# Third and fourth pass: gathered rows split into three bf16 parts on chip, summed by bf16 products

## The reference

```python
# layer 2 (third pass); ci, cj from the out and in degrees
msg = feat[src] * ci[src, None]
agg = segment_sum(msg, dst, N) * cj[:, None]
h = agg @ weight + bias
# layer 3 (fourth pass)
h = x @ W
msgs = h[src] * edge_weight[:, None]
y = segment_sum(msgs, dst, N) + bias        # then a layernorm with gamma, beta
```

## Time and profile before

| What | Value |
|---|---|
| time, median of 3 runs | 4434.95 us (4428.1 to 4437.35) |
| profiled execution, its span | 5246.3 us |
| first pass, first to last gather issue | 42.0 to 1410.5 us |
| second pass | 1471.2 to 2717.4 us |
| third pass | 2809.2 to 3997.5 us |
| fourth pass | 4024.9 to 5213.1 us |
| busy: PE, DVE, ACT, POOL | 52%, 38%, 26%, 61% of the span |

### The profile page before, as it was taken

How to read it: one execution, slowest core, us unless ns; L and a number is a source line. 1 busy time by engine, 2 the same in 40 slices (tenths; PEclk the granted TensorE clock), 3 DMA queues, 4 the chain that set the end, 5 groups by cost and what they waited for, 6 DMA issues and landing times.

```text
span 5246.3 us, 56090 instructions
## 1 busy us (share of the span) xinstructions
PE 2714.9 (52%) x15042; PEld 2473.5 (47%) x15042; DVE 1982.1 (38%) x4498; ACT 1353.8 (26%) x4318; POOL 3200.4 (61%) x3366
## 2 busy tenths in 40 slices
PE   6666676666756666566683543332334333333334
PEld 6666676666645555556552432222224222222234
DVE  3555545555655555555554111111113221122124
ACT  1121112222333333333343321211112121111113
POOL 4555555556356666666646666666665666666664
PEclk7676666767777777777785555555555555555555
DMA  7655555555433333333321111111112111111111
GB/s 193 156 142 140 148 137 139 149 143 144 125 94 85 81 84 83 82 83 83 83 60 42 35 35 35 35 35 35 35 35 46 35 36 34 35 35 34 35 35 44
DMA packets 337349, 409.90 MB, mean 78 GB/s; under 512 B 212224, under 2 KB 248691, under 8 KB 336957
## 3 DMA queue, kind: packets, MB, share of 16 engines
q0 software_dynamic: 133120, 245.58, 19.7%
q1 hardware_dynamic: 203933, 160.75, 11.7%
HBM read 386.26 MB, written 19.77 MB: 77 GB/s over the span
## 4 chain that ended last, share of the span: by engine, by line
another core or an unknown queue 32%; PE 19%; DVE 15%; POOL 14%; issue 14%; ACT 3%; DMA 1%; SPq 1%; ACTq 0%; DVEq 0%; POOLq 0%
POOL rows L563 14%; PE bank L655 10%; DVE same L1557 3%; DVE first_only L1256 2%; PE bank L669 2%; DVE first_only L1395 2%; DVE same L1256 2%; PE bank L668 1%; DVE prod L1325 1%; DVE score L1327 1%; DVE prod L1323 1%; PE bank L752 1%; DVE first_only L1264 1%; PE bank L759 1%
## 5 line engine op out<-in xcount | busy, mean ns | idle before, releaser
L655 PE MATMUL bank<-same,rows 128*96 128x128 f32 x4992 | 1059.8, 385 | 1468.8 <-issue 540.6
L655 PEld LDWEIGHTS bank<-same,rows 128*96 128x96 f32 x4992 | 917.5, 246 | 1593.7 <-issue 866.8
L563 POOL DMA_INDIRECT rows<-kv_table,src_idx x832 | 789.7, 949 | 610.0 <-DVE msg L1335 357.0
L563 POOL DMA_INDIRECT rows<-pair_table,src_idx x832 | 786.4, 945 | 520.5 <-issue 208.6
L563 POOL DMA_INDIRECT rows<-h_table,src_idx x832 | 788.7, 948 | 426.9 <-issue 235.0
L938 ACT COPY acc<-bank 96x511 f32 (+1 forms) x832 | 479.4, 576 | 2205.1 <-remote 1582.2
L563 POOL DMA_INDIRECT rows<-ci_table,src_idx x832 | 785.0, 943 | 412.6 <-issue 239.1
L1256 DVE TENSOR_TENSOR same<-bank,rank_col 128x512 f32<-128x512 f32 x624 | 420.6, 677 | 1000.7 <-remote 587.9
L1557 DVE TENSOR_SCALAR same<-iota_s,rank_col,src_hi 128x128 f32<-128x128 f32 x832 | 235.0, 359 | 906.7 <-remote 748.2
L655 PE MATMUL bank<-same,msg 128*105 128x128 f32 x1664 | 366.3, 391 | 384.5 <-ACT acc L940 362.7
L655 PEld LDWEIGHTS bank<-same,msg 128*105 128x105 f32 x1664 | 321.8, 268 | 398.2 <-DVE same L1256 200.9
(11 more groups left out here) (168 smaller groups left out, 2899.5 us busy)
## 6 DMA issues: line engine op xcount, KB each, us to landing
first_only<-in_attr_cols SPq DMA_DIRECT2D x104, 384.0 KB
first_only<-q_table SPq DMA_DIRECT2D x832, 48.0 KB
first_only<-rank_rows SPq DMA_DIRECT2D x104, 256.0 KB
first_only<-keep_rows SPq DMA_DIRECT2D x104, 192.0 KB
rows<-kv_table,src_idx POOLq DMA_INDIRECT x832
rows<-pair_table,src_idx POOLq DMA_INDIRECT x832
rows<-ci_table,src_idx POOLq DMA_INDIRECT x832
rows<-h_table,src_idx POOLq DMA_INDIRECT x832
```

The costliest lines, as they stand in the source:

```text
L563: pool.indirect_dma_start(rows[:, k, j, 0:width], None, table, bass.IndirectOffsetOnAxis(ap=src_idx[:, t:t + 1], axis=0)).then_inc(rows_in ...
L655: mm = pe.matmul(out[0:nrow, here], left(j), right(j), start=(j == 0), stop=(j == TQ - 1), skip_group_check=True)
```

## The change

In the third and fourth pass the float32 rows of a quad are split into three bf16 parts whose sum is the row: ACT copies the rows to bf16 (part 0), DVE subtracts part 0 from the rows in place, ACT copies what is left (part 1), DVE subtracts again into part 2. PE then makes three bf16 products a tile, twelve a quad, with a bf16 `same_b`, into the same bank. The last subtraction raises `split_done`, and POOL waits for that, not for `agg_done`. In the fourth pass DVE multiplies the rows by the edge weights first, and `same_b` is the plain 0/1 matrix made by one instruction. ACT's `spread` of a quad is moved behind the two copies of the next quad. `parts` and `same_b` lie in a region that only the first two passes use.

```diff
+        at = 0
+        parts = carve(2 * 3 * TQ * F // 2).bitcast(BF16).rearrange("p (k m j f) -> p k m j f", k=2, m=3, j=TQ)
+        same_b = carve(2 * TQ * P // 2).bitcast(BF16).rearrange("p (k j e) -> p k j e", k=2, j=TQ)
...
+        weighted, first_part, first_left, second_part, split_done = (
+            sem(n) for n in ("weighted", "first_part", "first_left", "second_part", "split_done"))
...
+                self.part = (n - 2) * NQ
...
-            edge_pass_pool(pool, ci_table, F, passes[2].agg_done)
+            edge_pass_pool(pool, ci_table, F, Signal(split_done, passes[2].part))
...
-            edge_pass_pool(pool, h_table, F, passes[3].agg_done)
+            edge_pass_pool(pool, h_table, F, Signal(split_done, passes[3].part))
...
                 wait(pe, s.same_done, q + 1)
-                wait(pe, rows_in[k], s.rows + (i + 1) * 16 * TQ)
+                wait(pe, split_done, s.part + q + 1)
                 wait(pe, s.copied, q - 1)
-                window(bank[2 + 2 * (k % 2)], F, at, lambda j: rows[:, k, j, 0:F], lambda j: same[:, k % 2, j, :]).then_inc(s.agg_done.sem, 1)
+                for j in range(TQ):
+                    here = bass.ds(at[j], P) if j else slice(0, P)
+                    for m in range(3):
+                        mm = pe.matmul(bank[2 + 2 * (k % 2)][0:F, here], parts[:, k % 2, m, j, :], same_b[:, k % 2, j, :],
+                                       start=(j == 0 and m == 0), stop=(j == TQ - 1 and m == 2), skip_group_check=True)
+                mm.then_inc(s.agg_done.sem, 1)
...
+            def split(s, q, i, k, ready_rows, value):
+
+                n = s.part + q
+                wait(act, ready_rows, value)
+                wait(act, s.agg_done, q - 1)
+                act.copy(parts[:, k % 2, 0], rows[:, k, :, 0:F]).then_inc(first_part, 1)
+                wait(act, first_left, n + 1)
+                act.copy(parts[:, k % 2, 1], rows[:, k, :, 0:F]).then_inc(second_part, 1)
...
+            def spread2(q, k):
+                spread(q, k, acc, F, bank[2 + 2 * (k % 2)], part_sum, s2.agg_done, s2.held, s2.copied)
...
                         act.copy(x_two_t[0:F, k % 2, :], bank[3][0:F, 0:P]).then_inc(u_cols, 1)
-                    spread(q, k, acc, F, bank[2 + 2 * (k % 2)], part_sum, s2.agg_done, s2.held, s2.copied)
+                    split(s2, q, i, k, rows_in[k], s2.rows + (i + 1) * 16 * TQ)
+                    if q > 0:
+                        spread2(q - 1, (k - 1) % GQ)
                     if static(q):
                         nodes4(q)
...
+            spread2(NQ - 1, GQ - 1)
...
                     q = i * GQ + k
+                    split(s3, q, i, k, weighted, q + 1)
                     if side_tile(q, kind):
                         wait(act, v_plus, q + 1)
                         act.activation(tile_row(x_nodes, q), x_plus[:, k % 2, :], ACT.Identity,
                                        bias=s_all[:, bass.ds(q, 1)]).then_inc(v_done, 1)
-                    spread(q, k, acc, F, bank[2 + 2 * (k % 2)], part_sum, s3.agg_done, s3.held, s3.copied)
+                    if q > 0:
+                        spread3(q - 1, (k - 1) % GQ)
                     if static(q):
                         nodes5(q)
 
...
+            spread3(NQ - 1, GQ - 1)
...
+            def split(s, q, k):
+
+                n = s.part + q
+                here = rows[:, k, :, 0:F]
+                wait(dve, first_part, n + 1)
+                dve.tensor_tensor(here, here, parts[:, k % 2, 0], ALU.subtract).then_inc(first_left, 1)
+                wait(dve, second_part, n + 1)
+                wait(dve, first_left, n + 1)
+                dve.tensor_tensor(parts[:, k % 2, 2], here, parts[:, k % 2, 1], ALU.subtract).then_inc(split_done, 1)
...
                     wait(dve, s2.agg_done, q - 1)
-                    one_hot(same[:, k % 2], iota_over, rank_col, q, P).then_inc(s2.same_done.sem, 1)
+                    one_hot(same_b[:, k % 2], iota_over, rank_col, q, P).then_inc(s2.same_done.sem, 1)
+                    split(s2, q, k)
...
                     wait(dve, s3.agg_done, q - 1)
-                    for j in range(TQ):
-                        at = bass.ds(q * TQ + j, 1)
-                        ins = dve.tensor_scalar(same[:, k % 2, j, :], iota_s[:], rank_col[:, at], weight_col[:, at], ALU.is_equal, ALU.mult)
-                    ins.then_inc(s3.same_done.sem, 1)
+                    one_hot(same_b[:, k % 2], iota_over, rank_col, q, P).then_inc(s3.same_done.sem, 1)
+                    wait(dve, rows_in[k], s3.rows + (i + 1) * 16 * TQ)
+                    dve.tensor_tensor(rows[:, k, :, 0:F], rows[:, k, :, 0:F], over(weight_col[:, q * TQ:(q + 1) * TQ], F), ALU.mult).then_inc(weighted, 1)
+                    split(s3, q, k)
```

More of the change, by code:

```diff
@@ L1131, in _, with spread3 @@
             s3 = passes[3]
+            def spread3(q, k):
+                spread(q, k, acc, F, bank[2 + 2 * (k % 2)], part_sum, s3.agg_done, s3.held, s3.copied)
             def nodes5(slot):
```

## The result

The changed kernel takes 4619.14 us (median, 4617.67 to 4619.91), where the kernel before takes 4436.15 beside it: a ratio of 1.0407, with a 95% interval of 1.0395 to 1.042. That is 183 us slower. I had forecast slower, 4566 us: the direction and the range held, and the loss is 52 us larger than the 131 I had added up.

What follows compares the result with a forecast made beforehand. POOL's gather issues at 1.25 us were taken as the bound. Side tiles 37, third-pass tail 45, fourth-pass tail 29 and DVE contention 20 sum to 131 us; 4435 + 131 = 4566 us, range 4470 to 4660 (forecast's own 4500 to 4630).

Steps and rivals of the forecast that it cites:

- The bound: All four passes: POOL's 3328 gather issues at 1.25 us, plus about 250 us around the passes, are the time.
- The stalls of 149 us a pass: Third and fourth pass: POOL stalls from late PE sums, 149 us each, said to belong only to the profiled execution.
- The split: Each quad of third and fourth pass: two ACT copies and two DVE subtractions, 2.24 us from rows to split_done.
- Side slots, +37: Third pass, 49 slots with side tiles: cycle grows from 4.0 to 6.0 us, +37 us, bounds +13 to +99.
- Tail of the third pass, +45: Last slots of the third pass: 9.5 us a slot instead of 5.56, +45 us, bounds +30 and +65.
- my 4.6 at its start: Third pass's tail: its first copy now waits for the next quad's rows, +4.6 us, included in the +45.
- Tail of the fourth pass, +29: Last slots of the fourth pass: 7.9 us a slot instead of 5.55, +29 us, bounds +12 and +45.
- POOL held up by DVE, +20: DVE operations with two SBUF inputs lengthen gather issues, mainly fourth pass: half of 39 us, +20, bounds 0 to 132.
- DVE and POOL collide in every quad: Rival, third and fourth pass: one or two 0.3 us losses a quad, 4650 to 4750 us, chance 0.15.
- 490 us: Case where all 880 new DVE operations block POOL for their whole 0.56 us, giving 5036 us, chance 0.02.
- Freeing the buffer early, "worth nothing": Third and fourth pass: releasing the buffer at split_done rather than PE's end gains nothing, as POOL did not wait in timed runs.

Runs made afterwards that it cites:

- e1: The kernel before, unchanged, profiled once more: 5256.54 us, with 5250.42 us as the median of seven other runs beside it.
- e9: Changed kernel with one bf16 product a quad instead of twelve in third and fourth pass, sums not formed: 4584.66 us, kernel before 4433.48.
- e2: Changed kernel with PE's side-tile product ahead of the quad's window in the third pass: 5578.08 us, kernel before 5250.42.
- e3: Changed kernel with node work on ACT and DVE one slot later, behind the next quad's split: 5532.05 us, 1.0536 of the kernel before.
- e10: e9 with the fourth pass's weighted rows also put in PSUM: 4561.42 us, 1.0289 of the kernel before.
- e6: Changed kernel with POOL waiting for agg_done again instead of split_done in both passes: 5350.39 us, 1.0196 of the kernel before.
- e8: The changed kernel run again, no edit: 5523.31 us, kernel before 5228.37, ratio 1.0567.
- e11: e9 plus a one-column ACT copy ahead of the split's first copy in the fourth pass: 4581.77 us, 1.034 of the kernel before.

## Why the prediction was right in sign and 52 us short

**The bound.** POOL's period is the time: right. The second pass took 1042 us, of which 832 issues at 1.25 make 1040.

**The stalls of 149 us a pass.** I used them rightly and named them wrongly. That timed runs issue without them, and that the sum is to be put on the median, held. That they "belong to the profiled execution" fell with e1: the seven runs beside it are as long. They come in some groups of runs and not in others. Each group ran on one chip, chips 13, 14 and 8 with late sums and chip 6 without, so chip and hour are not told apart.

**The split.** Forecast 2.24 us, measured 2.23 (2405.15 to 2407.38). A PE window forecast at 1.35 took 1.50.

**Side slots, +37.** Forecast cycle 6.0, measured 6.00, and 36 us of waits; e9 shortens the window in the chain and the third pass falls by 39 us. e2 shows the same chain by its order. Right.

**Tail of the third pass, +45.** 9.84 us a slot against my 9.5, and 105.5 us from the first product to the last against my 102, where 11 slots of 5.55 are 61: 44, and with my 4.6 at its start, which no run prices apart, 49. e3 shows that the order on ACT and DVE has a large part in it.

**Tail of the fourth pass, +29.** 7.81 to 7.85 against 7.9; 84.0 us against my 85, so 23, and 5 at its start: 28. Right.

**POOL held up by DVE, +20.** This is the step that failed, by its size: 67 us in the fourth pass, and as forecast next to nothing in the third (2.6 us on 10 issues). I wrote that one operation "in the fourth pass may meet it" 0.05 us ahead of a start. It does, 0.09 ahead. I then halved the term for doubt, priced a collision at 0.2 from the earlier trace rows, as if it were a constant, and left the weighting and the second subtraction, 16 of the 67 us, out of this count. It is an overlap. In the earlier trace rows DVE ended at 2676.83, 0.28 after the issue's start, and the issue was some 0.15 late; after, DVE ends at 3904.82, 0.47 after the start, and the issue is 0.34 late. In both the loss is what DVE still runs after the start, less 0.13. So it is in all 191 long issues of after (0.12 to 0.13) and in the 38 of before. By that rule the distance I had worked out gives 0.56 - 0.05 - 0.13 = 0.38 a quad, 196 x 0.38 = 74 us.

The price of a collision was thus to be had from the trace before, but not whether it happens. In after, 78 such operations of the third and fourth pass start 0 to 0.04 us ahead of an issue, and all but one cost it nothing; of 16 that start 0.04 to 0.05 ahead 7 lengthen it; all 186 that start 0.05 to 0.13 ahead do. The forecast distance of 0.05 lay on that edge, and measured it was 0.08 to 0.09. That 4619 still lies within the forecast's own 4500 to 4630, where contention was held to 0 to 40, is in part luck. The rival "DVE and POOL collide in every quad" (chance 0.15) was right for the fourth pass, at 0.35 us an issue, and wrong for the third.

The Trainium skill (SBUF — State Buffer, Who interferes with whom) has a DVE instruction with two SBUF inputs contend with a GpSimd instruction that reads SBUF. For the inputs e10 agrees: with two in SBUF the issues are 0.35 us late on average, with one in PSUM never. The Trainium skill (SBUF — State Buffer, Summary: rules for kernel authors) has the second one to issue block until the first finishes. That is a wait for what is left of the first, and not for the whole 0.56 us from which the prediction worked out 490 us. The traces agree, with 0.13 us less than the remainder, and with nothing lost where DVE began less than 0.04 us ahead.

**Freeing the buffer early, "worth nothing".** Without late sums there is no trace that tests it (e6 ran only with them). With them it is worse than nothing: 282 to 328 us over before in e8, e2 and e3, 100 in e6.

With measured sizes the sum is 36 + 49 + 28 + 67 = 180 of 183 us. The two tail terms are differences to slots of 5.55 us, read where sums come late, since the kernel before has no trace without late sums; no experiment without late sums took the tails away, so their 77 us are inferred from the slots and not shown as time. Read by stretches instead, after has 52 and 69 us more in the two passes than an unstalled 1042, 29 more between them than the earlier trace rows, and 12 more behind the last issue (45.7 us against 33.2): 162 in all. The other 21 us cannot be placed without a trace of before that has no late sums.

**Open.** Why the sums come late in one group of runs. What the traces show: the third pass of e1 is 146 us over an unstalled one. In the third pass of before and of e1 the signal arrived most often 4.3 to 4.4 us after POOL had stopped, in e8 3.3 to 3.7, in e6 about 2.9. Many stalls come six quads apart in before (8 PE records a quad) and most four apart in e6 (12 records): 48 records each. That would speak for a count of records, but in e8, with 12 records too, most are five quads or 60 records apart, and e9, which was to test it, met no late sums. The clock of PE does not tell the two apart there: the granted clock of the third and fourth pass is 0.50, the lower of its two levels (1.2 GHz), in after and in e8 alike. No kernel here was quicker than the one before.

## What to carry to other kernels

When one engine issues at a fixed period, place every new operation of its neighbour within that period by the distances in the trace; a fixed distance means the collision happens in every round or in none, so price it by the overlap times all rounds and do not halve it. Where the distance is within a few hundredths of a us of the edge, nothing and the full price are both open, and the range has to hold both. A step that is put behind another on an engine in program order is paid for in the places where that engine carries extra work (side tiles, tails), not in the steady part. And compare a trace's span with the timed median before its stalls are read: here 811 us of the first trace were in none of the timed runs.

## What was not expected of the hardware

- An indirect gather issue of 0.95 us becomes 1.29 to 1.33 us when a DVE `tensor_tensor` with both inputs in SBUF has started 0.05 to 0.09 us ahead of it (after, fourth pass). Started 0.01 us behind the issue (3903.10 after 3903.09), it costs the issue nothing and takes 0.58 us itself, not 0.56; started 0.03 to 0.04 us ahead, it takes 0.61 to 0.63 us and the issue still loses nothing (e11, 3904.09 and 3904.12).
- The same program takes 4433 us in one group of runs and 5250 us in another. A gather issue is as long on both (0.95 us) and so is a subtraction on DVE (0.56); the difference lies in waits for PE's signals, and PE's float32 product of the first pass (L662, L655 of before) has a mean of 386 to 395 ns where the signals come late and 346 to 349 where not. There the granted clock differs too: 0.68 in e8's first pass, 0.75 in after's.
